# Node attention of a four-layer decoder: the remainders of the rotary angles move from VectorE to GpSimd, ScalarE's folding and sines come a step later

## The chip, the cores and the metric

The kernel runs as one program on one core of a Trainium2 chip. The metric is the device time of one execution in microseconds (us), lower is better. All four compute engines (TensorE, VectorE, ScalarE, GpSimd) and the queue of SyncE run their own instruction streams and meet only at semaphores.

## The reference, cut to what matters

The whole kernel computes a decoder of four layers. The change touches the first attention only, a "node attention" with 16 heads of width 64, 4 groups of keys and values, and 4 nodes. Each token belongs to the 2 nodes of its head with the highest logits. For each node the rotary angle of a token is its count of earlier members times 32 frequencies:

```python
member = one_hot(top_k(x @ wr, 2)).sum(-2) > 0
pos = cumsum(member) - member              # per head and node
for n in range(4):
    c, s = cos(pos[n] * inv_freq), sin(pos[n] * inv_freq)
    qr = q * c + rotate_half(q) * s
    kr = k * c + rotate_half(k) * s
    scores = where(causal & member[n], qr @ kr.T * SCALE, NEG)
    outs.append(softmax(scores) @ v)
y = (softmax(top_k values) * outs at the two chosen nodes).sum()
```

The batch is 4 sequences of 256 tokens, so N = 1024 tokens, S = 256.

## The kernel before, in words

`l0_attn_heads` lays 4 nodes times 32 frequencies on the 128 partitions and the 1024 tokens on the free axis. So a head needs one table of cosines and one of sines, each 128x1024 f32, and both are kept twice (`h % 2`). The loop runs over STEPS = 64 steps, s = 4h + b: head h, sequence b. Every engine has a loop over s of its own, written out by hand, and semaphores that count steps tie them together.

The angles of a head h >= 2 come about in five pieces:

- `turns(h)` (ScalarE, L991): positions times frequency, in full turns, into `cosines`. It is issued at b == 2 of head h - 2, when the tables of that parity are no longer read.
- `reduce_turns(h)` (VectorE, L1063 and L1065): the nearest whole number by adding and subtracting a constant, and the signed remainder, into `sines`. Issued behind `combine` at b == 3 of head h - 2.
- `fold(h)` (ScalarE, L996): absolute value into `cosines`. Issued at b == 3 of head h - 2.
- `sines_of(h)` (ScalarE, L1000 and L1001): two passes of the sine, which need another activation table than the exponents do. Issued at b == 0 of head h - 1.
- The readers: `rotate_q` (VectorE, L1072 to L1082) two steps ahead of the step it serves, so first at b == 2 of head h - 1, and `rotate_k` (GpSimd, L1135 to L1138), which may run up to two steps ahead of the scores. Both wait for `trig_ready`.

In a step s the other work is: VectorE `find_top(s)` (L1088), `rotate_q(s+2)`, `combine(s)` (L1094 to L1105); TensorE `score(s+1)` (L908 to L918, which waits for `combined` of step s - 1, for the rotated keys and the query slots), `weigh(s-2)`, `turn(s-1)` (L928), `project_q(s+3)` (L894); ScalarE `exponents(s)` (L1009), `copy_out(s-2)` (L1024), `copy_turned(s-1)` (L1018). In the last head of a group of four (heads 3, 7 and 11) each step has a K chunk besides: TensorE `project_k` (L886) before `project_q`, and ScalarE `copy_k` (L980), which must be done before TensorE's one projection bank is free for `project_q`.

GpSimd had nothing but `rotate_k`: four instructions a step, of which two are 128x512 and two 128x256.

Of the kernel before, what the change touches and what calls it, by code (L numbers as in the profile page):

```python
# [66 lines left out]
class Core:  # L67
# [12 lines left out]
    def sb(self, name, shape, dt=F32, ctx=None):  # L80
        return (ctx or self.ctx).enter_context(self.nc.sbuf_tensor(name, shape, dt))
# [487 lines left out]
H0, KV0, D0, NODES, CHOICES = 16, 4, 64, 4, 2  # L569
# [3 lines left out]
ROUND = 1.5 * 2.0 ** 23  # L573
# [183 lines left out]
def l0_attn_heads(k, W, values, mix, absent_t, chosen_t, pos_t, heads_t):  # L757
# [3 lines left out]
    nc = k.nc  # L761
# [4 lines left out]
    step = lambda s: divmod(s, B)  # L766
# [9 lines left out]
    with ExitStack() as ctx:  # L776
# [15 lines left out]
        cosines, sines = sb("cosines", [P, 2, N]), sb("sines", [P, 2, N])  # L792
# [25 lines left out]
        with nc.Block() as block:  # L818
# [154 lines left out]
            @block.scalar  # L973
            def _(act):
                def copy_k(chunk):
                    g, (part, half) = chunk // 4, K_CHUNKS[chunk % 4]
                    act.wait_ge(projected_ready, place["k", chunk] + 1)
                    if g >= 1:
                        act.wait_ge(k_rotated, G0 * B * g - 2 + 2 * half)
                    nc.scalar.activation(k_both[:, part, half * BANK:(half + 1) * BANK],  # L980
                                         k_place(chunk), ACT.Copy, scale=D0 ** -0.5)\
                        .then_inc(k_copied, 1)

                def turns(h):
                    if h < 2:
                        act.wait_ge(positions_spread, h + 1)
                    if h >= 2:
                        act.wait_ge(pos_loaded, 64 * (h - 1))
                        act.wait_ge(q_taken, B * (h - 1))
                        act.wait_ge(k_rotated, B * (h - 1))  # L990
                    nc.scalar.activation(cosines[:, h % 2], scores[:, h] if h < 2 else pos[:], ACT.Copy, scale=W("freq"))\  # L991
                        .then_inc(turns_ready, 1)

                def fold(h):
                    act.wait_ge(turns_reduced, h + 1)
                    nc.scalar.activation(cosines[:, h % 2], sines[:, h % 2], ACT.Abs).then_inc(turns_folded, 1)  # L996

                def sines_of(h):
                    act.wait_ge(turns_folded, h + 1)
                    nc.scalar.activation(sines[:, h % 2], sines[:, h % 2], ACT.Sin, scale=-TWO_PI)  # L1000
                    nc.scalar.activation(cosines[:, h % 2], cosines[:, h % 2], ACT.Sin, scale=-TWO_PI,  # L1001
                                         bias=k.quarter_turn[:]).then_inc(trig_ready, 1)

                def exponents(s):
                    for i in range(TB):
                        act.wait_ge(topped, 2 * s + i + 1)
                        for slot in range(CHOICES):
                            one = unit(scores, s, i)[:, slot]
                            last = nc.scalar.activation(one, one, ACT.Exp,  # L1009
                                                        bias=top[:, s % 2, i, slot:slot + 1],  # L1010
                                                        accum_out=total[:, s % 2, i, slot:slot + 1])
                        last.then_inc(exp_ready, 1)

                def copy_turned(s):
                    act.wait_ge(turned_ready, s + 1)
                    if s >= 2:
                        act.wait_ge(out_ready, s - 1)
                    nc.scalar.copy(probs_t[:, s % 2], turned[:, 0:P + S]).then_inc(turned_copied, 1)  # L1018

                def copy_out(s):  # L1020
                    h, b = step(s)
                    part, of = (slice(x % 2 * D0, (x % 2 + 1) * D0) for x in (h, h // G0))
                    act.wait_ge(out_ready, s + 1)
                    nc.scalar.copy(heads_t[part, h // 2, b * S:(b + 1) * S], out_ps[of, s % 2, :])\  # L1024
                        .then_inc(out_copied, 1)

                turns(0)
                turns(1)
                copy_k(0)
                fold(0)  # L1030
                copy_k(1)
                sines_of(0)
                copy_k(2)
                copy_k(3)
                fold(1)
                sines_of(1)
                for s in range(STEPS):
                    h, b = step(s)
                    exponents(s)
                    if s >= 2:  # L1040
                        copy_out(s - 2)
                    if s >= 1:
                        copy_turned(s - 1)
                    if k_chunk_at(s) is not None:
                        copy_k(4 * (s // (G0 * B) + 1) + k_chunk_at(s))
                    if b == 0 and 1 <= h < H0 - 1:
                        sines_of(h + 1)
                    if b == 2 and h + 2 < H0:
                        turns(h + 2)
                    if b == 3 and h + 2 < H0:  # L1050
                        fold(h + 2)
                copy_turned(STEPS - 1)
                copy_out(STEPS - 2)
                copy_out(STEPS - 1)

            @block.vector
            def _(v):
                link = k.vchain

                def reduce_turns(h):  # L1060

                    v.wait_ge(turns_ready, h + 1)
                    link(v, nc.vector.tensor_scalar(sines[:, h % 2], cosines[:, h % 2], ROUND, ROUND, ALU.add,  # L1063
                                                    ALU.subtract))
                    nc.vector.tensor_tensor(sines[:, h % 2], sines[:, h % 2], cosines[:, h % 2], ALU.subtract)\  # L1065
                        .then_inc(turns_reduced, 1)
# [18 lines left out]
                def find_top(s):  # L1085
                    for i in range(TB):
                        v.wait_ge(scores_ready, 2 * s + i + 1)
                        nc.vector.tensor_reduce(top[:, s % 2, i], unit(scores, s, i), AX.X, ALU.max, negate=True)\  # L1088
                            .then_inc(topped, 1)
# [23 lines left out]
                for s in range(STEPS):  # L1113
                    h, b = step(s)
                    find_top(s)
                    if s + 2 < STEPS:
                        rotate_q(s + 2)
                    combine(s)
                    if b == 3 and h + 2 < H0:
                        reduce_turns(h + 2)  # L1120

            @block.gpsimd
            def _(g):
                link = k.gchain

                def rotate_k(s):
                    h, b = step(s)
                    g.wait_ge(k_copied, 4 * (h // G0) + (2 if b < 2 else 4))
                    g.wait_ge(trig_ready, h + 1)
                    if s >= 1:  # L1130
                        g.wait_ge(k_rotated, s)
                    if s >= 2:
                        g.wait_ge(scores_ready, 2 * (s - 1))
                    source = k_both[:, :, of_batch(s)]
                    nc.gpsimd.tensor_tensor(k_part[:], source, at_batch(sines, s), ALU.mult)  # L1135
                    link(g, nc.gpsimd.tensor_tensor(k_rot[:, s % 2], source, at_batch(cosines, s), ALU.mult))  # L1136
                    nc.gpsimd.tensor_tensor(k_rot[:, s % 2, 0], k_rot[:, s % 2, 0], k_part[:, 1], ALU.subtract)  # L1137
                    nc.gpsimd.tensor_tensor(k_rot[:, s % 2, 1], k_rot[:, s % 2, 1], k_part[:, 0], ALU.add).then_inc(k_rotated, 1)  # L1138

                k.gchain(g, nc.gpsimd.memset(spread[:], 0.0))  # L1140
                for h in range(2):
                    nc.gpsimd.affine_select(out=spread[:, h], in_=spread[:, h], compare_op=ALU.not_equal, fill=1.0,
                                            base=-NODES * h, pattern=[[-1, NODES], [0, FREQS]], channel_multiplier=1)\
                        .then_inc(spread_set, 1)
                for s in range(STEPS):
                    rotate_k(s)

# [2408 lines left out]
```

## Time and profile before

| what | value |
|---|---|
| median of 3 runs | 1866.5 us (1866.48 to 1873.33) |
| profiled execution, its own time | 1868.13 us |
| its span, first to last instruction | 1866.4 us |
| busy share of the span | PE 74%, DVE 59%, ACT 38%, POOL 24% |
| stage of the 16 heads | about 38 to 498 us |
| busy in that stage (460.5 us) | PE 394.2, DVE 410.6, ACT 267.4, POOL 267.1 |

The stage is about a quarter of the span. Engine names in the rows: PE is TensorE, PEld its weight loads, DVE VectorE, ACT ScalarE, POOL GpSimd, SP SyncE. A time in brackets behind a row is how long the engine stood idle before it, and who released it. PEclk is the granted TensorE clock as a share of 2.4 GHz. In rows with an x count, start is that of the first and the length covers them all.

### The profile page before, as it was taken

The numbers are of one execution on the slowest core, as the hardware profiler recorded it, in microseconds if no ns is written. First come the engines' busy times: TensorE is split into PE (matmuls) and PEld (weight loads), VectorE is DVE, ScalarE is ACT, GpSimd is POOL, SyncE is SP. The second block draws the span as 40 slices with busy tenths as digits, with TensorE's granted clock in tenths as the row PEclk, the third lists the DMA queues.
The fourth block names the chain that finished last, engine by engine and source line by source line (L and its number), as shares of the span: only waits on it lengthen the run. The fifth ranks groups of instructions, "written<-read, shape, count | busy, mean of one in ns | idle before, by whom it ended". The sixth has DMA issues, their size and how long they took to land. (4 is left out here: it accounts for less than half of the span.)

```text
span 1866.4 us, 25316 instructions
## 1 busy us (share of the span) xinstructions
PE 1387.0 (74%) x9045; PEld 1055.8 (57%) x9045; DVE 1109.8 (59%) x2340; ACT 709.0 (38%) x1529; POOL 443.9 (24%) x464
## 2 busy tenths in 40 slices
PE   4898898888866897774765956758616878869785
PEld 3676666666745564561444955546513756646663
DVE  5899999999446577224566545352454827425534
ACT  4456666656222464221321221013203333634351
POOL 2565566565210100120101310000001015002300
PEclk8899899998878799786887977669868989989897
DMA  6111111010010100430002500000200002000100
GB/s 217 28 35 36 27 41 35 27 41 15 1 58 1 35 1 1 141 116 0 1 13 101 181 17 1 1 1 1 88 3 1 1 1 43 2 0 18 27 2 12
DMA packets 31612, 64.01 MB, mean 34 GB/s; under 512 B 6784, under 2 KB 18176, under 8 KB 30976
## 3 DMA queue, kind: packets, MB, share of 16 engines
q1 hardware_dynamic: 30464, 60.15, 10.4%
q0 software_dynamic: 1024, 2.23, 0.5%
q8 instruction: 74, 1.21, 0.3%
q14 instruction: 50, 0.41, 0.1%
HBM read 54.13 MB, written 4.18 MB: 31 GB/s over the span
## 5 line engine op out<-in xcount | busy, mean ns | idle before, releaser
L188 POOL TENSOR_TENSOR rstd<-spread,minus_half 128x4 f32<-128x4 f32 x36 | 36.9, 1024 | 913.2 <-DVE spread L170 913.2
L918 PE MATMUL l0h_scores<-l0h_k_rot,l0h_q_slots 128*128 128x128 f32 (+1 forms) x1024 | 208.2, 351 | 0.0
L918 PEld LDWEIGHTS l0h_scores<-l0h_k_rot,l0h_q_slots 128*128 128x128 f32 x1024 | 171.2, 210 | 13.3
L1135 POOL TENSOR_TENSOR l0h_k_part<-large_weights,l0h_sines 128x512 f32<-128x512 f32 x64 | 84.0, 1313 | 177.8 <-PE l0h_scores L918 129.8
L1009 ACT ACTIVATE l0h_scores<-l0h_scores,l0h_top 128x128 f32<-128x128 f32 (+1 forms) x256 | 100.6, 393 | 26.3 <-DVE l0h_top L1088 26.2
L1082 DVE TENSOR_TENSOR l0h_q_slots<-l0h_q_rot,l0h_chosen 128x1024 f32<-128x1024 f32 x64 | 78.4, 1225 | 6.7
L894 PE MATMUL l0h_projected<-XT,l0h_wq 128*128 128x256 f32 x256 | 70.1, 397 | 15.8 <-ACT large_weights L980 11.8
L1136 POOL TENSOR_TENSOR l0h_k_rot<-large_weights,l0h_cosines 128x512 f32<-128x512 f32 x64 | 81.0, 1266 | 0.0
L908 PE MATMUL l0h_scores<-l0h_key_masks,l0h_query_picks 4*128 4x128 bf16 (+1 forms) x256 | 45.2, 258 | 47.7 <-DVE l0h_probs L1105 47.7
L1447 ACT ACTIVATE l0n_probs<-l0n_scores,l0n_top 128x256 f32<-128x256 f32 x128 | 53.9, 483 | 38.9 <-DVE l0n_top L1478 38.7
L1088 DVE TENSOR_REDUCE l0h_top<-l0h_scores 128x2 f32<-128x256 f32 (+1 forms) x128 | 65.0, 546 | 5.4 <-PE l0h_scores L918 5.4
L1024 ACT COPY l0a_heads_t<-l0h_out_ps 64x256 f32<-64x256 f32 x64 | 23.5, 367 | 116.9 <-PE l0h_out_ps L939 116.6
L894 PEld LDWEIGHTS l0h_projected<-XT,l0h_wq 128*128 128x128 f32 x256 | 44.6, 194 | 32.6 <-ACT large_weights L980 22.6
L908 PEld LDWEIGHTS l0h_scores<-l0h_key_masks,l0h_query_picks 4*128 4x128 bf16 x256 | 14.1, 93 | 80.4 <-DVE l0h_probs L1105 64.7
L1138 POOL TENSOR_TENSOR l0h_k_rot<-l0h_k_rot,l0h_k_part 128x256 f32<-128x256 f32 x64 | 57.4, 896 | 0.0
L1009 ACT ACTIVATION_READ_ACCUMULATOR l0h_scores<-l0h_scores,l0h_top 128x1 f32 x256 | 52.5, 205 | 0.0
L1072 DVE TENSOR_TENSOR l0h_q_part<-l0h_projected,l0h_sines 128x512 f32<-128x512 f32 x64 | 43.6, 682 | 14.3 <-PE l0h_projected L894 13.8
L1137 POOL TENSOR_TENSOR l0h_k_rot<-l0h_k_rot,l0h_k_part 128x256 f32<-128x256 f32 x64 | 50.1, 784 | 5.0
L1101 DVE TENSOR_SCALAR l0h_probs<-l0h_scores,l0h_share 128x128 f32<-128x128 f32 (+1 forms) x128 | 47.6, 413 | 2.3
L1105 DVE SCALAR_TENSOR_TENSOR l0h_probs<-l0h_scores,l0h_share,l0h_probs 128x128 f32<-128x128 f32 (+1 forms) x128 | 47.5, 413 | 2.3
L2124 POOL DMA_INDIRECT l1e_rows<-l1f_rows,l1e_token_int x16 | 25.6, 1602 | 85.8 <-DVE l1e_token_int L2234 85.2
L1478 DVE TENSOR_REDUCE l0n_top<-l0n_scores 128x4 f32<-128x1024 f32 x32 | 39.1, 1222 | 10.7 <-PE l0n_scores L1399 10.5
(761 smaller groups left out, 3703.6 us busy)
## 6 DMA issues: line engine op xcount, KB each, us to landing
l1e_experts<-in_l_experts SPq DMA_DIRECT2D x16, 768.0 KB, 4.3
l0e_experts<-in_l_experts SPq DMA_DIRECT2D x15, 578.0 KB, 3.9
l0h_chosen<-l0h_chosen_dram SPq DMA_DIRECT2D x64, 128.0 KB, 3.0
small_weights<-in_w_l_ffn SPq DMA_DIRECT2D x1, 4016.0 KB, 12.2
l0h_pos<-l0h_pos_dram SPq DMA_DIRECT2D x56, 64.0 KB, 2.1
large_weights<-in_w_l_xattn SPq DMA_DIRECT2D x1, 2632.0 KB, 9.1
l3f_late<-l3f_values SPq DMA_DIRECT2D x2, 1040.0 KB, 7.0
l0h_wq<-in_l_wq SPq DMA_DIRECT2D x16, 128.0 KB, 3.0
```

The lines of the kernel that those rows point to most:

```text
L894: mm = nc.tensor.matmul(out[:, part * S:(part + 1) * S], wq[:, h % 2, part * P:(part + 1) * P], k.XT[:, b * S:(b + 1) * S], start=True, st ...
L908: nc.tensor.matmul(at[:, slot], query_picks[:, h % 2, slot, query], key_masks[:, h % 2, b * S:b * S + KEYS[i][1]], start=(slot == 0), stop ...
L918: mm = nc.tensor.matmul(at[:, slot], q_slots[:, s % 2, slot, part, i * P:(i + 1) * P], k_rot[:, s % 2, part, 0:KEYS[i][1]], start=False, s ...
L1009: last = nc.scalar.activation(one, one, ACT.Exp, bias=top[:, s % 2, i, slot:slot + 1], accum_out=total[:, s % 2, i, slot:slot + 1])
L1082: nc.vector.tensor_tensor(q_slots[:, s % 2], bc(q_rot[:].unsqueeze(1), [P, CHOICES, 2, S]), chosen_of(s), ALU.mult).then_inc(slots_ready, 1)
L1088: nc.vector.tensor_reduce(top[:, s % 2, i], unit(scores, s, i), AX.X, ALU.max, negate=True)\
L1101: last = nc.vector.tensor_scalar(prob(i), unit(scores, s, i)[:, 0], share[:, s % 2, i, 0:1], None, ALU.mult)
L1135: nc.gpsimd.tensor_tensor(k_part[:], source, at_batch(sines, s), ALU.mult)
L1136: link(g, nc.gpsimd.tensor_tensor(k_rot[:, s % 2], source, at_batch(cosines, s), ALU.mult))
L1137: nc.gpsimd.tensor_tensor(k_rot[:, s % 2, 0], k_rot[:, s % 2, 0], k_part[:, 1], ALU.subtract)
L1138: nc.gpsimd.tensor_tensor(k_rot[:, s % 2, 1], k_rot[:, s % 2, 1], k_part[:, 0], ALU.add).then_inc(k_rotated, 1)
L1447: last = nc.scalar.activation(probs[:, u % 2, o, i], scores[:, u % 2, o, i], ACT.Exp, bias=top[:, u % 2, o, i:i + 1])
```

## The change

Three things move, and nothing is computed differently.

- `reduce_turns` goes from VectorE to GpSimd. It was issued at b == 3 of head h - 2 for head h; now it is issued behind `rotate_k(4(h-1))`, so at b == 0 of head h - 1 in GpSimd's own loop. Heads 0 and 1 stay on VectorE.
- ScalarE's `fold` is issued at b == 0 of head h - 1, where the sines were.
- ScalarE's `sines_of` is issued at b == 1 of head h - 1.

`turns` stays at b == 2 of head h - 2, and all waits keep their counts. For each of the heads 2 to 15 the same instructions run, 14 times in all. In GpSimd's queue `rotate_k(4(h-1)+1)` and all that follows stand behind the two new instructions and their wait for `turns_ready`.

```diff
--- before.py
+++ after.py
@@ -1044,11 +1044,11 @@
                     if k_chunk_at(s) is not None:
                         copy_k(4 * (s // (G0 * B) + 1) + k_chunk_at(s))
                     if b == 0 and 1 <= h < H0 - 1:
+                        fold(h + 1)
+                    if b == 1 and 1 <= h < H0 - 1:
                         sines_of(h + 1)
                     if b == 2 and h + 2 < H0:
                         turns(h + 2)
-                    if b == 3 and h + 2 < H0:
-                        fold(h + 2)
                 copy_turned(STEPS - 1)
                 copy_out(STEPS - 2)
                 copy_out(STEPS - 1)
@@ -1116,8 +1116,6 @@
                     if s + 2 < STEPS:
                         rotate_q(s + 2)
                     combine(s)
-                    if b == 3 and h + 2 < H0:
-                        reduce_turns(h + 2)
 
             @block.gpsimd
             def _(g):
@@ -1137,13 +1135,22 @@
                     nc.gpsimd.tensor_tensor(k_rot[:, s % 2, 0], k_rot[:, s % 2, 0], k_part[:, 1], ALU.subtract)
                     nc.gpsimd.tensor_tensor(k_rot[:, s % 2, 1], k_rot[:, s % 2, 1], k_part[:, 0], ALU.add).then_inc(k_rotated, 1)
 
+                def reduce_turns(h):
+                    g.wait_ge(turns_ready, h + 1)
+                    link(g, nc.gpsimd.tensor_scalar(sines[:, h % 2], cosines[:, h % 2], ROUND, ROUND, ALU.add, ALU.subtract))
+                    nc.gpsimd.tensor_tensor(sines[:, h % 2], sines[:, h % 2], cosines[:, h % 2], ALU.subtract)\
+                        .then_inc(turns_reduced, 1)
+
                 k.gchain(g, nc.gpsimd.memset(spread[:], 0.0))
                 for h in range(2):
                     nc.gpsimd.affine_select(out=spread[:, h], in_=spread[:, h], compare_op=ALU.not_equal, fill=1.0,
                                             base=-NODES * h, pattern=[[-1, NODES], [0, FREQS]], channel_multiplier=1)\
                         .then_inc(spread_set, 1)
                 for s in range(STEPS):
+                    h, b = step(s)
                     rotate_k(s)
+                    if b == 0 and 1 <= h < H0 - 1:
+                        reduce_turns(h + 1)
```

## Rows read from the trace of the kernel before

**Rows 1.** The page's first line: span, and instructions of all engines.
```profile
span 1866.4 us, 25316 instructions
```

**Rows 2.** Windows: 13 heads; one head with K chunks; the next (start:end, length, busy, PEclk).
```profile
98.62:464.18 365.56, 318.30 (x1742) 243.03 (x1741) 337.26 (x704) 224.02 (x610) 218.94 (x208) 0.94 0.11 32
238.89:266.41 27.52, 24.37 (x138) 18.04 (x137) 26.01 (x56) 17.93 (x48) 16.92 (x16) 1.00 0.12 35
266.41:295.25 28.84, 24.77 (x142) 18.62 (x141) 25.44 (x55) 18.00 (x48) 16.92 (x17) 1.00 0.11 34
```

**Rows 3.** Timeline of VectorE, steps 26 to 28 (start, length, engine, line, operation, tiles).
```profile
238.89 0.18 DVE L1094 RECIPROCAL l0h_scores<-l0h_total 128x4 f32<-128x4 f32 x1
...
245.06 0.18 DVE L1094 RECIPROCAL l0h_scores<-l0h_total 128x4 f32<-128x4 f32 x1
...
246.91 0.84 DVE L1063 TENSOR_SCALAR l0h_sines<-l0h_cosines 128x1024 f32<-128x1024 f32 x1
...
247.78 1.63 DVE L1065 TENSOR_TENSOR l0h_sines<-l0h_sines,l0h_cosines 128x1024 f32<-128x1024 f32 x1
...
250.26 0.67 DVE L1072 TENSOR_TENSOR l0h_q_part<-l0h_projected,l0h_sines 128x512 f32<-128x512 f32 x1
...
253.66 0.18 DVE L1094 RECIPROCAL l0h_scores<-l0h_total 128x4 f32<-128x4 f32 x1
```

**Rows 4.** Timeline of TensorE, a plain step, then a step with a K chunk.
```profile
240.88 0.28 PE L908 MATMUL l0h_scores<-l0h_key_masks,l0h_query_picks 4*128 4x128 bf16 x2
...
241.21 1.06 PE L918 MATMUL l0h_scores<-l0h_k_rot,l0h_q_slots 128*128 128x128 f32 x8
...
245.02 0.49 PE L928 MATMUL l0h_turned<-ident,l0h_probs 128*128 128x128 f32 x3
...
245.35 1.03 PE L894 MATMUL l0h_projected<-XT,l0h_wq 128*128 128x256 f32 x4
...
247.04 0.28 PE L908 MATMUL l0h_scores<-l0h_key_masks,l0h_query_picks 4*128 4x128 bf16 x2 [0.67 <-DVE l0h_probs L1105]
...
267.03 0.49 PE L928 MATMUL l0h_turned<-ident,l0h_probs 128*128 128x128 f32 x3
...
269.07 1.13 PE L894 MATMUL l0h_projected<-XT,l0h_wq 128*128 128x256 f32 x4 [0.69 <-ACT large_weights L980]
```

**Rows 5.** Timeline of ScalarE: turns, copies, the sines and what follows them.
```profile
240.49 1.15 ACT L991 ACTIVATE l0h_cosines<-l0h_pos,large_weights 128x1024 f32<-128x1024 bf16 x1
...
245.62 0.48 ACT L1018 COPY l0h_probs_t<-l0h_turned 128x384 f32<-128x384 f32 x1
...
268.42 0.60 ACT L980 ACTIVATE large_weights<-l0h_projected 128x512 f32<-128x512 f32 x1 [0.31 <-PE l0h_projected L886]
...
282.61 1.28 ACT L1000 ACT_TABLE_LOAD   x1
...
284.87 1.13 ACT L1001 ACTIVATE l0h_cosines<-l0h_cosines,quarter_turn 128x1024 f32<-128x1024 f32 x1
...
289.06 0.37 ACT L1024 COPY l0a_heads_t<-l0h_out_ps 64x256 f32<-64x256 f32 x1
```

**Rows 6.** Timeline of GpSimd: one set of rotated keys, and one under the remainders.
```profile
233.77 1.27 POOL L1135 TENSOR_TENSOR l0h_k_part<-large_weights,l0h_sines 128x512 f32<-128x512 f32 x1 [6.24 <-PE l0h_scores L918]
...
237.03 0.73 POOL L1138 TENSOR_TENSOR l0h_k_rot<-l0h_k_rot,l0h_k_part 128x256 f32<-128x256 f32 x1
...
248.29 1.71 POOL L1138 TENSOR_TENSOR l0h_k_rot<-l0h_k_rot,l0h_k_part 128x256 f32<-128x256 f32 x1
```

**Rows 7.** Groups by line and shape, GpSimd, whole span (busy us, mean ns | idle before).
```profile
L2354 POOL MEMSET l2a_values<- 128x7168 f32 x1 | 6.1, 6077 | 12.6 <-POOLq L256 12.6
```

**Rows 8.** Windows: a pause of TensorE in head 6 and the time after it.
```profile
225.40:228.31 2.91, 0.00 (x1) 0.00 (x1) 2.81 (x8) 2.88 (x4) 2.05 (x3) 1.00 0.00 0
228.30:233.80 5.50, 5.49 (x24) 4.25 (x25) 5.19 (x12) 3.79 (x10) 0.03 (x1) 0.69 0.01 5
```

**Rows 9.** Waits of VectorE, 84 to 480 us (us in total, times, longest us).
```profile
DVE l0h_q_part L1072 <- PE l0h_projected L894: 8.5, 11, 1.2
```

## The prediction

> **What bounds the kernel now.** I read the page first for the span [rows 1]; the profiled execution took 1868.1 us, 1.7 more than its span and 1.6 above the median of the runs. The change touches only the 16 heads, so I cut that stage into heads by the windows. From step 6 to step 58, thirteen heads, takes 365.56 us, 28.1 a head. The heads whose last steps carry K chunks (3, 7, 11) take 27.5 each and the ones behind them (4, 8, 12) 28.8 [rows 2], so the other seven take (365.56 - 3 x 27.5 - 3 x 28.8) / 7 = 28.1.
>
> Then the timeline of VectorE, which is busy 337 of those 366 us [rows 2]. I take L1094, the first instruction of `combine`, as the mark of a step and write M(s) for its start. M(26) to M(27) is 6.17 us with no gap: a plain step is VectorE's own work. M(27) to M(28) is 8.60 [rows 3]: the two remainder instructions stand in it. They cost 2.42 us net there, although their own lengths sum to 2.47. Four plain steps and one reduction are 24.68 + 2.42 = 27.1; the other 1.0 of the 28.1 is waiting.
>
> Part of that 1.0 is TensorE's clock. While VectorE reduces, TensorE has nothing to do, and in head 6 it pauses for 2.91 us; in the 5.5 us after the pause its granted clock is 0.69 on the mean, so for (1 - 0.69) / 0.5, about 3.4 us, of it 1.2 GHz [rows 8]. Its projections then come late to `rotate_q`, which waits 8.5 us in 11 waits over the stage [rows 9].
>
> The other engines have slack in a plain step. TensorE needs 5.50 us from the scores to the end of `project_q` (240.88 to 246.38) and then waits 0.67 for `combine` [rows 4]. GpSimd stood idle for 6.24 us before a `rotate_k` of 3.99 us (233.77 to 237.76) [rows 6].
>
> **What is removed.** 14 reductions leave VectorE. If nothing else became late, that is 14 x 2.42 = 34 us. GpSimd gets back little: under VectorE's reduction its L1138 took 1.71 instead of 0.73 [rows 6], beside slack.
>
> **What is added on GpSimd.** Two instructions over 128x1024, which no row shows on that engine. The second has two inputs: L1135 takes 1.27 for 512 columns and L1138 0.73 for 256 [rows 6], so 0.54 per 256 and 0.73 + 3 x 0.54 = 2.35 for 1024. The first has one input: at least as long as a mere write, 6.08 us for 7168 columns or 0.87 for 1024 [rows 7], at most as long as the two-input one, 2.35. I take 1.5, between them. With 0.1 for the link, X = 3.95, call it 4.0, between 3.3 and 4.8.
>
> The Trainium skill's GPSIMD Engine Reference, section Engine selection, advises against such work on this engine: two-input operations are about twice as slow there, while one-input ones run at roughly line rate. The two-input half agrees with the trace, 1.27 on GpSimd against 0.67 for VectorE's 128x512 (L1072). By the one-input half, at that page's 1.2 GHz and one column a cycle, an estimate for the first instruction is 0.85 us and X is 3.3, which would make the sum below about 1858.
>
> **Where it lies: the new chain.** I walk one plain head from M(4h-2) = 0, in the steady state where the sines of the head before came just before it.
>
> 1. ScalarE. The sines end when `rotate_q` can start, 3.4 before the mark (L1072 to L1094, 250.26 to 253.66 [rows 3]). The table load and four exponents end 3.06 later (286.00 to 289.06 [rows 5]), at -0.35; two copies end at 0.5 and `turns` (1.15 [rows 5]) at 1.65.
> 2. GpSimd finished `rotate_k(4h)` at about 0.6 and waits for `turns`. The reduction runs from 1.7 to 5.7, `rotate_k(4h+1)` (4.0) ends at 9.8.
> 3. TensorE would start the key products of `score(4h+1)` at 6.17 + 1.98 + 0.33 = 8.5 (245.06 to 247.04 [rows 3, 4], 240.88 to 241.21 [rows 4]). It waits 1.3. From there to the end of `project_q(4h+3)` is 5.17 (241.21 to 246.38 [rows 4]): 14.97. `rotate_q(4h+3)` wants it at M(4h) + 2.77 = 15.1 (2.77 is 6.17 - 3.40). Just in time: M(4h+1) = 18.5, where before it was 20.9.
> 4. TensorE starts `score(4h+2)` at 14.97 (it could from 14.3) and `turn(4h)` 4.14 later (240.88 to 245.02 [rows 4]), at 19.1. ScalarE's copy ends 1.1 behind that (245.02 to 246.10 [rows 4, 5]) at 20.2. The sines take 3.39 (282.61 to 286.00 [rows 5]) and end at 23.6.
> 5. `rotate_q(4h+4)` on VectorE wanted them at M(4h+1) + 2.77 = 21.3. It waits 2.3, and M(4h+2) = 23.6 + 0.05 + 3.4 = 27.05.
>
> So of the 2.42 that the reduction gives back, about 2.3 is taken by a new wait of L1072 for the sines. The chain closes on itself (mark, turns, remainders, keys, scores, turned probabilities, sines, mark) with a period of 23.05 + X: each us on GpSimd is a us of the head. `fold` (1.06 by the same kind of row) now lies between copies and exponents at about 15 to 16; the exponents end near 17.9, before M(4h+1), so it costs nothing. It would cost if the scores came 0.7 later.
>
> TensorE pauses here too: `project_q(4h+1)` ends at -3.4 + 1.3 + 1.03 = -1.1 and the next scores start at 1.98, a pause of 3.1, no shorter than the 2.91 that was followed by the low clock [rows 8]. So I leave the low clock in. Where it lasts 7 us it delays step 3 by 0.6 to 0.8; where it lasts 3.4 us GpSimd's delay covers it. Mean 0.4: a plain head is 27.45 against 28.1.
>
> **Heads with K chunks.** There a TensorE step is longer by 1.81: from `turn` to the end of the projections 3.17 (267.03 to 270.20) for 1.36 (245.02 to 246.38) [rows 4]. It falls once on step 3, which then also holds up `rotate_q(4h+3)` by 1.8, and the copy of the chunk ends 1.99 behind the start of `turn` (267.03 to 269.02 [rows 4, 5]) for 1.08, so 0.9 more stands ahead of the sines in step 4. The chain is 27.05 + 1.81 + 0.9 = 29.75, with 0.3 for the clock 30.05. Before it was 27.5: there TensorE's long step lay under VectorE's reduction and there was no pause. The heads behind them start with chunks still in steps 2 and 3 (`turns` at 2.3, 0.65 later) but without the 3 us pause: 27.6 against 28.84 [rows 2].
>
> **The sum.** Plain heads, eight with head 1: 8 x (27.45 - 28.1) = -5.2, and +1.0 because head 1 starts without the early `turns` of item 1. Heads 3, 7, 11: 3 x (30.05 - 27.5) = +7.6. Heads 4, 8, 12: 3 x (27.6 - 28.84) = -3.7. A last pause behind head 14: +0.8. Sum +0.5, so the profiled execution would take 1868.6 and the median about 1867 us. With X at 3.3 it is about 14 x 0.7 = 10 less, 1857; with 4.8 it is 14 x 0.8 = 11 more, 1878. The remaining slacks are a few tenths, so half a us a head, 7 us, is my error of the walk itself.
>
> **The rivals.** Effects within 0.5% (9.3 us) can't be told from no change here.
>
> - The forecast, gains and losses cancel, 1867: 0.5, its own range 1860 to 1874.
> - The chain binds less than I think, because the one-input instruction runs at the pace of a write (X 3.3): about 1857. For it: nothing in the instruction needs a second read. Against: two-operation arithmetic is more than a write. 0.15.
> - VectorE stays the bound and all of 34 us comes back: 1833. That needs X under about 1.7, less than the two-input instruction alone. 0.05.
> - GpSimd is slower than I take it, one-input work no faster than two-input or slower: X 4.8 or more, 1878 or more. It decides from X = 4.6. 0.15.
> - The low clock falls on the chain. In step 3 and 4 TensorE's work is 9.3 us of the 27; the 3.4 us of half clock seen in rows 8 cost 1.7 us of work when they lie on it. In the 11 heads with the pause, 11 x 1.7 = 19: 1886. For it: the wait of 1.3 in step 3 makes a second pause. Against: the first pause ends 8 us before the key products, and the second is short. 0.15.
>
> Faster by over 0.5% takes the 0.05, most of the 0.15 at 1857 and a little of the forecast: 0.2. Slower by over 0.5% takes both slow cases: 0.28. The rest, 0.52, is the same. The range 1856 to 1882 holds the forecast, both ends of X and the milder part of the clock's case.
>
> **What would show it.** In the trace after: L1063 and L1065 for heads 2 on stand on POOL, with lengths near 1.5 and 2.35; POOL's wait for L991 ahead of them; L1072 waiting for ACT L1001 about 2.3 us, 14 times, longer in heads 3, 7 and 11; L918 waiting for POOL L1138 about 1.3; L1094 to L1094 at 6.17 but for the step at b == 2 (and b == 1 in the chunk heads); heads of 27.5, of 30 and of 27.6. I am wrong if L1072 doesn't wait for the sines, if X is outside 3.3 to 4.8, or if PEclk in the stage falls well under 0.94.

## The result, and the profile after

The changed kernel took 1912.9 us (median of 4 runs, 1908.7 to 1917.5) beside 1869.9 for the kernel before (1866.5 to 1876.0). The ratio is 1.0227, with a 95% interval of 1.0186 to 1.0267: 2.3% slower, where no change was forecast and the range ended at 1882. Of the runs below, one execution of e11 took 2479.5 us at a granted clock of 0.55; it is in no ratio.

The spans differ by 40.5 us (1866.4 and 1906.9). From M(2) to M(58), the marks between which the moved work lies, the kernel before took 394.2 us and the changed one 433.3: 39.1 of the 40.5 are there. So there is nothing to look for outside the 16 heads. Behind M(63), the mark of the last step, nothing differs between the kernels below, and yet their profiled executions took from 1372.9 to 1381.5 us there; a difference of a few us is therefore read between the marks.

The groups of GpSimd in the changed kernel (mean ns of one behind the busy time; line numbers of `rotate_k` moved to L1133 to L1136):

```profile
L1133 POOL TENSOR_TENSOR l0h_k_part<-large_weights,l0h_sines 128x512 f32<-128x512 f32 x64 | 81.0, 1265 | 133.3 <-ACT l0h_cosines L1001 104.8 <-PE l0h_scores L918 23.7 <-POOL l0h_k_rot L1136 4.8
...
L1140 POOL TENSOR_SCALAR l0h_sines<-l0h_cosines 128x1024 f32<-128x1024 f32 x14 | 50.8, 3631 | 17.7 <-ACT l0h_cosines L991 17.7
...
L1141 POOL TENSOR_TENSOR l0h_sines<-l0h_sines,l0h_cosines 128x1024 f32<-128x1024 f32 x14 | 32.9, 2349 | 1.2
```

The two-input instruction is as predicted, 2.35 us. The one-input instruction takes 3.63 us, not 1.5, and lies outside the bounds of 0.87 and 2.35. X is 6.06, from 196.91 to 202.97 in the next rows, and not 4.0.

One plain head of the changed kernel in the timeline, M(18) to M(22), to be read against the walk and against [rows 3 to 6]:

```profile
195.37 0.18 DVE L1094 RECIPROCAL l0h_scores<-l0h_total 128x4 f32<-128x4 f32 x1
195.68 1.15 ACT L991 ACTIVATE l0h_cosines<-l0h_pos,large_weights 128x1024 f32<-128x1024 bf16 x1
...
196.91 3.63 POOL L1140 TENSOR_SCALAR l0h_sines<-l0h_cosines 128x1024 f32<-128x1024 f32 x1 [0.95 <-ACT l0h_cosines L991]
...
200.62 2.35 POOL L1141 TENSOR_TENSOR l0h_sines<-l0h_sines,l0h_cosines 128x1024 f32<-128x1024 f32 x1
...
206.18 0.72 POOL L1136 TENSOR_TENSOR l0h_k_rot<-l0h_k_rot,l0h_k_part 128x256 f32<-128x256 f32 x1
206.95 1.16 PE L918 MATMUL l0h_scores<-l0h_k_rot,l0h_q_slots 128*128 128x128 f32 x8 [2.09 <-POOL l0h_k_rot L1136]
...
208.48 3.29 PE L918 MATMUL l0h_scores<-l0h_k_rot,l0h_q_slots 128*128 128x256 f32 x8
...
211.81 0.69 DVE L1088 TENSOR_REDUCE l0h_top<-l0h_scores 128x2 f32<-128x512 f32 x1 [1.66 <-PE l0h_scores L918]
213.95 0.69 DVE L1072 TENSOR_TENSOR l0h_q_part<-l0h_projected,l0h_sines 128x512 f32<-128x512 f32 x1 [1.44 <-PE l0h_projected L894]
214.17 1.06 PE L918 MATMUL l0h_scores<-l0h_k_rot,l0h_q_slots 128*128 128x128 f32 x8
...
215.60 1.89 PE L918 MATMUL l0h_scores<-l0h_k_rot,l0h_q_slots 128*128 128x256 f32 x8
217.98 0.49 PE L928 MATMUL l0h_turned<-ident,l0h_probs 128*128 128x128 f32 x3
...
219.08 1.28 ACT L1000 ACT_TABLE_LOAD   x1
...
221.33 1.13 ACT L1001 ACTIVATE l0h_cosines<-l0h_cosines,quarter_turn 128x1024 f32<-128x1024 f32 x1
...
222.57 0.69 DVE L1072 TENSOR_TENSOR l0h_q_part<-l0h_projected,l0h_sines 128x512 f32<-128x512 f32 x1 [2.35 <-ACT l0h_cosines L1001]
...
225.98 0.18 DVE L1094 RECIPROCAL l0h_scores<-l0h_total 128x4 f32<-128x4 f32 x1
```

The chain of the prediction is there link by link: mark, `turns` (ended at 1.5 after the mark, forecast 1.65), GpSimd waiting for it, the remainders, the keys, TensorE waiting for the keys, the sines behind the turned probabilities, and L1072 waiting 2.35 us for them (forecast 2.3). Two links are longer than in the walk: the remainders, and TensorE. From the start of the key products to the end of the scores it took 4.8 us (206.95 to 211.77), where the same matmuls of the next step took 3.3 (214.17 to 217.49), and L1088 waited for it. The windows say why (columns as in [rows 2]):

```profile
69.70:503.00 433.30, 362.74 (x1880) 274.34 (x1878) 333.43 (x729) 240.33 (x658) 300.73 (x252) 0.91 0.10 29
...
202.43:204.86 2.43, 2.43 (x15) 1.71 (x13) 2.32 (x6) 1.55 (x7) 2.43 (x3) 1.00 0.00 0
...
206.95:213.04 6.09, 6.09 (x27) 5.00 (x28) 3.78 (x9) 0.29 (x1) 4.99 (x5) 0.72 0.01 4
```

Before the pause of 2.09 us the granted clock is 1.00; in the 6.1 us behind it 0.72 on the mean, so a good half of them at 1.2 GHz. In the kernel before the clock fell once in a plain head, beside VectorE's work. Here it falls on the chain, at the wait for keys, in 11 of the 14 heads by windows of 2 us. Head 6 is the one plain head where it stayed at 1.00 there, behind a wait of 2.05 us that ended at 237.56:

```profile
235.98:237.98 2.00, 0.41 (x3) 0.42 (x4) 1.79 (x4) 0.44 (x2) 1.69 (x4) 1.00 0.00 0
237.98:239.98 2.00, 2.00 (x15) 1.56 (x14) 1.89 (x6) 0.00 (x0) 2.00 (x2) 1.00 0.00 0
```

It took 28.9 us, the other seven 30.3 to 31.0. The fall behind the first pause of a head, which head 6 has like the others (0.50 from 229.98 to 231.98), so cost it nothing: the chain without low clock is 23.05 + 6.06 = 29.1.

The waits between 84 and 480 us (us in total, times, longest), where the kernel before had 8.5 us in all for L1072 [rows 9]:

```profile
DVE l0h_q_part L1072 <- ACT l0h_cosines L1001: 33.2, 13, 3.3
...
PE l0h_scores L918 <- POOL l0h_k_rot L1136: 23.5, 12, 2.3
DVE l0h_q_part L1072 <- PE l0h_projected L894: 22.1, 16, 3.0
DVE l0h_top L1088 <- PE l0h_scores L918: 20.6, 12, 3.2
```

VectorE waits 33.2 us for the sines, 22.1 for projections and 20.6 for scores; the 14 x 2.42 = 34 us that it no longer works don't cover these.

### The profile page after: what moved, and what is told of

It is laid out like the page before. It is cut to its first block and busy times, and to the rows that moved or that the text cites. A ratio compares the mean times of both kernels' runs of the same rounds, so it can differ in the third digit from the quotient of the medians.

```text
span 1906.9 us, 25316 instructions
## 1 busy us (share of the span) xinstructions
PE 1408.0 (74%) x9045; PEld 1068.6 (56%) x9045; DVE 1080.3 (57%) x2312; ACT 707.8 (37%) x1529; POOL 509.1 (27%) x492
## 5 line engine op out<-in xcount | busy, mean ns | idle before, releaser
L188 POOL TENSOR_TENSOR rstd<-spread,minus_half 128x4 f32<-128x4 f32 x36 | 36.9, 1024 | 913.7 <-DVE spread L170 913.7
L918 PE MATMUL l0h_scores<-l0h_k_rot,l0h_q_slots 128*128 128x128 f32 (+1 forms) x1024 | 223.6, 369 | 29.1 <-POOL l0h_k_rot L1136 29.1
L918 PEld LDWEIGHTS l0h_scores<-l0h_k_rot,l0h_q_slots 128*128 128x128 f32 x1024 | 180.3, 219 | 48.5 <-POOL l0h_k_rot L1136 31.7
L1133 POOL TENSOR_TENSOR l0h_k_part<-large_weights,l0h_sines 128x512 f32<-128x512 f32 x64 | 81.0, 1265 | 133.3 <-ACT l0h_cosines L1001 104.8
L1009 ACT ACTIVATE l0h_scores<-l0h_scores,l0h_top 128x128 f32<-128x128 f32 (+1 forms) x256 | 100.9, 395 | 33.1 <-DVE l0h_top L1088 32.9
L1088 DVE TENSOR_REDUCE l0h_top<-l0h_scores 128x2 f32<-128x256 f32 (+1 forms) x128 | 66.2, 550 | 27.4 <-PE l0h_scores L918 27.4
L1072 DVE TENSOR_TENSOR l0h_q_part<-l0h_projected,l0h_sines 128x512 f32<-128x512 f32 x64 | 44.1, 689 | 64.8 <-ACT l0h_cosines L1001 35.5
L1454 ACT ACTIVATE l0n_probs<-l0n_scores,l0n_top 128x256 f32<-128x256 f32 x128 | 53.8, 483 | 39.1 <-DVE l0n_top L1485 39.0
L1140 POOL TENSOR_SCALAR l0h_sines<-l0h_cosines 128x1024 f32<-128x1024 f32 x14 | 50.8, 3631 | 17.7 <-ACT l0h_cosines L991 17.7
L1009 ACT ACTIVATION_READ_ACCUMULATOR l0h_scores<-l0h_scores,l0h_top 128x1 f32 x256 | 52.8, 206 | 0.0
L1135 POOL TENSOR_TENSOR l0h_k_rot<-l0h_k_rot,l0h_k_part 128x256 f32<-128x256 f32 x64 | 46.4, 725 | 5.0
L1136 POOL TENSOR_TENSOR l0h_k_rot<-l0h_k_rot,l0h_k_part 128x256 f32<-128x256 f32 x64 | 46.4, 725 | 0.0
## 6 DMA issues: line engine op xcount, KB each, us to landing
small_weights<-in_w_l_ffn SPq DMA_DIRECT2D x1, 4016.0 KB, 12.2
```

The lines of the kernel that those rows point to most:

```text
L918: mm = nc.tensor.matmul(at[:, slot], q_slots[:, s % 2, slot, part, i * P:(i + 1) * P], k_rot[:, s % 2, part, 0:KEYS[i][1]], start=False, s ...
L1009: last = nc.scalar.activation(one, one, ACT.Exp, bias=top[:, s % 2, i, slot:slot + 1], accum_out=total[:, s % 2, i, slot:slot + 1])
L1140: link(g, nc.gpsimd.tensor_scalar(sines[:, h % 2], cosines[:, h % 2], ROUND, ROUND, ALU.add, ALU.subtract))
L1454: last = nc.scalar.activation(probs[:, u % 2, o, i], scores[:, u % 2, o, i], ACT.Exp, bias=top[:, u % 2, o, i:i + 1])
```

## The experiments

Three questions: is it the length of the remainders or their place; how much is ScalarE's later place; and is the 1.4 us per head above 23.05 + 6.07 the clock? All ratios below are against the kernel before, run beside them on the same chip. Its medians were 1872.7 (e1 to e4), 1875.0 (e5 to e8) and 1873.6 (e9 to e11).

**e1, the rounding left out.** This kernel does not compute the rounding, and all its remainders are 0.

```diff
-link(g, nc.gpsimd.tensor_scalar(sines[:, h % 2], cosines[:, h % 2], ROUND, ROUND, ALU.add, ALU.subtract))
-nc.gpsimd.tensor_tensor(sines[:, h % 2], sines[:, h % 2], cosines[:, h % 2], ALU.subtract)\
+nc.gpsimd.tensor_tensor(sines[:, h % 2], cosines[:, h % 2], cosines[:, h % 2], ALU.subtract)\
     .then_inc(turns_reduced, 1)
```

> The changed kernel with the first GpSimd instruction (the rounding, 3.63 us) left out and the second one subtracting the angles from themselves, so all remainders are 0: the rounding is not computed. The chain theory (a head lasts 23.05 us plus the time X of the remainders on GpSimd, and the low clock comes on top) has X fall from 6.07 to 2.4 us. GpSimd is then early enough for the scores and TensorE's own order sets the sines: heads of 26.5 to 27 instead of 30.6, so about 50 us less than the changed kernel, near 1862. Rival, the sines' later place alone is the loss: X does not matter, 1905 to 1913. Rival, the low clock is the loss: the pauses before score(4h+4) stay, a gain of at most 15, about 1897.

Measured: 1861.5 us, ratio 0.9947 (0.9928 to 0.9967), 1862 forecast. Plain heads take 26.4 to 26.8 us. The one remaining instruction took 1.90 us, less than 2.35; both its inputs are the same tile. The length of the remainders on GpSimd is what separates the changed kernel from a gain of 0.5%: with short remainders there, the later sines don't make it slow.

**e2, the rounding as two instructions.**

```diff
-link(g, nc.gpsimd.tensor_scalar(sines[:, h % 2], cosines[:, h % 2], ROUND, ROUND, ALU.add, ALU.subtract))
+link(g, nc.gpsimd.tensor_scalar(sines[:, h % 2], cosines[:, h % 2], ROUND, None, ALU.add))
+link(g, nc.gpsimd.tensor_scalar(sines[:, h % 2], sines[:, h % 2], ROUND, None, ALU.subtract))
```

> The changed kernel with the rounding on GpSimd as two instructions, one that adds and one that subtracts, where before one instruction did both. If GpSimd's time in one-input arithmetic goes by operations (two in the 3.63 us), each takes about 1.8 and nothing changes: 1908 to 1916. If one operation runs at the pace of a write (0.87 to 1.0 us), X falls by about 1.6 us, and by the chain theory 14 x 1.6 = 22 us go: about 1890. If the cost goes by instruction, whatever it does, it is 3.6 each and X rises by 3.6: about 1960.

Measured: 1949.9 us, ratio 1.0415 (1.0385 to 1.0444). None of the three forms fits; it is nearest to a cost by instruction. The groups of this kernel, GpSimd:

```profile
L1140 POOL TENSOR_SCALAR l0h_sines<-l0h_cosines 128x1024 f32<-128x1024 f32 x14 | 38.8, 2774 | 17.6 <-ACT l0h_cosines L991 17.6
L1141 POOL TENSOR_SCALAR l0h_sines<-l0h_sines 128x1024 f32<-128x1024 f32 x14 | 38.8, 2774 | 1.2
```

One operation with a constant takes 2.77 us, the two in one instruction 3.63: the second operation costs 0.86 and the rest of the instruction 1.9. X is about 8.1 here, 2.0 more than in the changed kernel, and 14 x 2.0 = 28 of the 37 us follow from it. No run separated the rest; the granted clock from M(2) to M(58) is 0.87 here and 0.91 in the changed kernel.

**e3, ScalarE's part alone.** On the kernel before, VectorE reducing at b == 3:

```diff
                     if b == 0 and 1 <= h < H0 - 1:
+                        fold(h + 1)
+                    if b == 1 and 1 <= h < H0 - 1:
                         sines_of(h + 1)
...
-                    if b == 3 and h + 2 < H0:
-                        fold(h + 2)
```

> ScalarE's part alone: remainders on VectorE at b == 3 as in the kernel before, fold at b == 0 and sines at b == 1. The walk gives the sines ready at 25.4 us after the mark where rotate_q wants them at 23.7: L1072 waits 1.7 in every head, heads of about 28.9 instead of 28.1, 10 us slower than the kernel before, about 1878. Rival, GpSimd's time is the whole loss and ScalarE's place costs nothing: 1866 to 1870. Rival, ScalarE's later place is most of the loss: 1900 or more.

Measured: 1903.7 us, ratio 1.0163 (1.0137 to 1.0189), three times the forecast loss, and where the rival stood by which ScalarE's later place is most of the loss (1900 or more). The wait is the forecast one but longer, in this kernel's list of waits (98 to 500 us):

```profile
DVE l0h_q_part L1072 <- ACT l0h_cosines L1001: 36.5, 14, 4.5
```

That is 2.6 a head for 1.7. At 187.14 us, in a head where the clock was full, the wait is 1.68, as walked; in others it is up to 4.5. A part that I had not seen: `rotate_k` of the next head now starts with the late sines and so falls on VectorE's reduction. L1065 takes 1.84 us on the mean instead of 1.50, and the step with the reduction 9.0 to 9.6 in ten of the 14 heads; in the kernel before it was 8.6 in nine of them [rows 3]. So ScalarE's half costs 30 us when VectorE keeps the remainders, while e1, with the same place of the sines and no reduction on VectorE, is faster than the kernel before: what the later sines cost depends on which engine has the remainders.

**e4, the second keys first.** The same instructions, one place later in GpSimd's loop:

```diff
                     rotate_k(s)
-                    if b == 0 and 1 <= h < H0 - 1:
+                    if b == 1 and 1 <= h < H0 - 1:
                         reduce_turns(h + 1)
```

> The changed kernel with the remainders behind the second set of rotated keys of the head (b == 1 in GpSimd's loop) instead of the first. Same instructions, same total time on GpSimd. The chain theory: the keys of step 4h+1 are ready before TensorE wants them, the remainders end at about 10.7 us after the mark, long before the fold at 16, and the keys of step 4h+2 are just in time. The remainders leave the chain: heads of 26.5 to 27, about 50 us less than the changed kernel, near 1860, so below the kernel before. Rival, what counts is how much GpSimd has to do: 1905 to 1913. Rival, the delay moves on to the keys of step 4h+2: 1885 to 1900.

Measured: 1861.7 us, ratio 0.9949 (0.9926 to 0.9973), 1860 forecast. Since GpSimd does the same work for the same 6.07 us, the loss needs the place of it too: in front of the keys that TensorE wants next. Of VectorE's large waits in the changed kernel only the one for the sines is left (84 to 480 us):

```profile
DVE l0h_q_part L1072 <- ACT l0h_cosines L1001: 29.1, 14, 3.3
DVE l0h_q_part L1072 <- PE l0h_projected L894: 7.6, 9, 1.3
...
DVE l0h_top L1088 <- PE l0h_scores L918: 0.8, 3, 0.3
```

**e5, and the sines ahead of the copies.** On e4, in ScalarE's loop:

```diff
                     exponents(s)
+                    if b == 1 and 1 <= h < H0 - 1:
+                        sines_of(h + 1)
                     if s >= 2:
                         copy_out(s - 2)
...
-                    if b == 1 and 1 <= h < H0 - 1:
-                        sines_of(h + 1)
```

> e4 with one thing more: at b == 1 ScalarE issues the sines right behind the exponents, ahead of copy_out and copy_turned, so that they no longer wait for TensorE's scores and turned probabilities. In e4 L1072 still waits 1.8 us for the sines in each head (27.4 us in 13 waits). The chain theory: the sines end about 2.4 us earlier, before L1072 wants them, and a plain head falls from 26.7 to 24.7 to 25.3, four plain steps of VectorE: 20 to 28 us less than e4, about 1837. Rival, the copies that now come behind the sines hold up TensorE and the turned probabilities, and the wait only moves there: no gain, 1855 to 1865.

Measured: 1834.4 us, ratio 0.9786 (0.9758 to 0.9815), 1837 forecast: 2.1% faster than the kernel before, and the best of all. VectorE's timeline over one head has no gap:

```profile
198.34 0.17 DVE L1094 RECIPROCAL l0h_scores<-l0h_total 128x4 f32<-128x4 f32 x1
...
204.51 0.17 DVE L1094 RECIPROCAL l0h_scores<-l0h_total 128x4 f32<-128x4 f32 x1
...
223.04 0.17 DVE L1094 RECIPROCAL l0h_scores<-l0h_total 128x4 f32<-128x4 f32 x1
```

Each step of this head is 6.17 or 6.18 and a plain head 24.7, VectorE's own work, which the rival at 1833 stood for; it is reached here with X at 6.07, because X is off the chain. The granted clock from M(2) to M(58) is 1.00, and TensorE's longest pause there is 0.8 us.

**e6, the sines early with the remainders left in place.** The edit of e5 on the changed kernel.

> The changed kernel with the sines right behind the exponents at b == 1, and the remainders left where the change put them. The chain then runs turns, remainders (6.07), keys (4.1), scores of step 4h+1 (3.3), copies, fold and exponents (4.9), sines (3.4), rotate_q: about 27 us instead of 29.1, and less of it is TensorE's: about 45 us less than the changed kernel, 1865 to 1875. Rival, TensorE's late scores set the head whatever ScalarE does: 1900 or more.

Measured: 1906.0 us, ratio 1.0175 (1.0146 to 1.0205): my forecast missed by 30 us, and the rival holds. L1072 no longer waits for the sines, and TensorE's wait for keys grows to up to 3.5:

```profile
PE l0h_scores L918 <- POOL l0h_k_rot L1136: 41.9, 13, 3.5
DVE l0h_top L1088 <- PE l0h_scores L918: 41.3, 13, 3.8
DVE l0h_q_part L1072 <- PE l0h_projected L894: 29.5, 22, 3.0
```

I had closed the chain over the sines, but a shorter loop lies inside it: mark, `turns`, remainders, keys, scores, projection, `rotate_q(4h+3)`, and then a plain step to the next mark. With early sines `turns` also ends 2.0 after the mark instead of 1.5, since VectorE no longer waits for the sines just before the mark. The keys come 12.2 after the mark, so this loop is 12.2 + 5.17 + 3.4 + 6.17 = 26.9. Plain heads take 28.7 where the clock is at 0.5 for about 3.5 us behind the wait for keys, and 30.1 to 30.2 where it is for about 7: half of that time more, as TensorE's share of the loop runs at half speed.

**e7 and e9, the pauses filled.** Matmuls whose result nobody reads, on the changed kernel:

```diff
+def fill(n, copied):
+    pe.wait_ge(turned_copied, copied)
+    for _ in range(n):
+        nc.tensor.matmul(turned[:, P + S:BANK], k.ident[:], k.ident[:], start=True, stop=True, ...)
...
+                        if i == 0 and b == 1 and h >= 1:      # e9: h % 4 in (1, 2)
+                            fill(14, s - 2)                   # e9: fill(9, s - 2)
                         if i == 0:
                             pe.wait_ge(k_rotated, s + 1)
...
+                    if s % B == B - 1 and 1 <= s // B < H0 - 1:   # e9: the same heads
+                        fill(12, s - 1)
                     if s + 1 < STEPS:
                         score(s + 1)
```

> The changed kernel with useless matmuls into unused columns of the turned bank: 12 before the scores of each step 4h+4, 14 before the key products of each step 4h+1, in the pauses of TensorE. They compute nothing that is used. If the 1.4 us by which heads exceed 23.05 + 6.07 = 29.1 are the low clock, the granted clock in the stage rises from 0.91 to nearly 1.0 and heads fall to about 29.2: some 15 us less, 1895 to 1900. Rival, the 1.4 us are a wait that the walk missed: clock up and time unchanged, 1908 to 1916.

> e7 with the useless matmuls in the plain heads alone (1, 2, 5, 6, 9, 10, 13, 14) and 9 instead of 14 before the key products of step 4h+1, so that they end before the keys do. In e7 plain heads fell from about 30.6 to 29.47, with the 14 ending 0.65 us behind the keys, and the other heads rose. If the low clock is what plain heads have above 23.05 + 6.07, they take 29.0 to 29.4 here and the whole is 8 x 1.2, some 10 us, less than the changed kernel: 1900 to 1905. Rival, the gain in plain heads is eaten in the heads behind them: 1908 to 1916.

e7: 1910.3 us, ratio 1.0203 (1.0170 to 1.0237), not to be told from the changed kernel, though its granted clock rose from 0.91 to 1.00. By the whole time the rival would have it. The heads say otherwise. Head lengths, worked out as the difference of the starts of L1094 at b == 2, means:

```
                         plain (8)   3, 7, 11   4, 8, 12
changed kernel             30.4        32.1       31.4
e7, 14 and 12 everywhere   29.4        32.0       32.6
e9, 9 and 12 in plain      29.0        32.6       31.4
```

In e7 the matmuls take about 8 us off the eight plain heads and add 4 in heads 4, 8 and 12; from M(2) to M(58) e7 is 3.9 us shorter than the changed kernel (429.4), and behind M(58) 4 us longer, 1.8 of them in the last head, which hides it in the whole time. e9 leaves them out in the other heads and takes 1900.8 us, ratio 1.0146 (1.0113 to 1.0179), as forecast, with plain heads at 29.0 where the chain without low clock gives 29.1. The low clock is 1.4 us of a plain head of the changed kernel.

**e8, the sines at b == 0 again.**

```diff
-                    if b == 1 and 1 <= h < H0 - 1:
+                    if b == 0 and 1 <= h < H0 - 1:
                         sines_of(h + 1)
```

> The changed kernel with ScalarE's sines put back to b == 0, behind the fold, GpSimd as in the change. By the walk the fold ends at about 18.3 us, the sines at 21.7 and the exponents of step 4h+1 behind the second table load at 24.8, which VectorE wants at 18.5 to 20.5: the exponents become the wait in place of L1072, heads of 31 to 32, slower than the changed kernel by 10 to 20, about 1925. Rival, the later place of the sines is what the change loses: then this gains 20 or more, under 1890.

Measured: 1965.0 us, ratio 1.0494 (1.0457 to 1.0530), in the forecast direction but 40 us more. The exponents became the wait (L1094 for L1009, 36.9 us in 11), and TensorE waited longer for keys (49.9 us in 12), with the clock at 0.84 between 100 and 460 us. With the remainders on GpSimd where the change put them, the later place of the sines is needed.

**e10, the walk at a size within its bounds.** Rounding and remainders are not computed here; two instructions of a length between the bounds stand in their place.

```diff
-link(g, nc.gpsimd.tensor_scalar(sines[:, h % 2], cosines[:, h % 2], ROUND, ROUND, ALU.add, ALU.subtract))
-nc.gpsimd.tensor_tensor(sines[:, h % 2], sines[:, h % 2], cosines[:, h % 2], ALU.subtract)\
+link(g, nc.gpsimd.tensor_tensor(sines[:, h % 2], cosines[:, h % 2], cosines[:, h % 2], ALU.subtract))
+nc.gpsimd.tensor_tensor(sines[:, h % 2], sines[:, h % 2], cosines[:, h % 2], ALU.mult)\
```

> The changed kernel with two two-input instructions on GpSimd in place of the rounding and the difference: a subtraction of the angles from themselves (1.90 us in e1) and a product (2.35), so X is 4.35 and all remainders are 0 (rounding and remainders are not computed). This is the prediction's walk at a size inside its own bounds. If only the size of X was wrong, its sum holds here: 1867 + 14 x 0.35, about 1872, heads of 27.4 to 27.9. If the low clock on TensorE's share of the chain was missed as well, plain heads are 28.5 to 29 and the time 1882 to 1890.

Measured: 1873.1 us, ratio 0.9999 (0.9978 to 1.0021), with 1.90 and 2.36 us on GpSimd. Heads took 27.8 (plain), 30.3 (3, 7, 11) and 27.7 (4, 8, 12); the walk with 0.35 more has 27.8, 30.4 and 27.95. The prediction's sum holds where its size does, though the 27.8 is in part luck: it is the mean of six plain heads at 26.9 to 27.2, below the chain's 27.4 without low clock, and of heads 1 and 13 at 30.6 and 28.8. In these two and in head 7 TensorE waited 1.2 to 1.8 us for keys and the granted clock fell to 0.5; so the last rival's case turned up in three heads even with X in its bounds. The walk also makes this kernel 5 us slower than the kernel before, and the two were alike (1873.1 and 1873.6).

**e11, without GpSimd.** ScalarE's order of e5 with the remainders on VectorE.

> The kernel before with ScalarE's part of e5 alone: fold at b == 0, sines at b == 1 right behind the exponents; the remainders stay on VectorE at b == 3. A plain head is then 4 x 6.17 + 2.42 = 27.1 plus what the low clock costs, against 24.7 in e5: 1855 to 1865, so that the remainders on GpSimd, behind the second set of keys, are worth 25 us of e5. Rival, the order on ScalarE is the whole gain of e5: 1835 to 1842.

Measured: 1865.4 us, ratio 0.9963 (0.9945 to 0.9982), at the edge of the forecast 1855 to 1865. Plain heads are mostly 27.3, so the move to GpSimd in the right place is worth 31 us of e5 (1865.4 less 1834.4).

## Why the prediction was wrong, point by point

**The step that failed** is the bound in "What is added on GpSimd": the one-input instruction "at most as long as the two-input one, 2.35". It measured 3.63. X was 6.06 and not 4.0, and 14 x 2.1 = 29 of the 43 us follow from it by the prediction's own rule, that each us on GpSimd is a us of the head. In e10, with X inside the bounds, the rest of the sum comes out as far as the heads show it, with the luck told there. That upper bound had no row behind it; here the instruction with fewer inputs was the longer one. The Trainium skill's GPSIMD Engine Reference, section Engine selection, has one-input work at roughly line rate. The estimate of 0.85 us from it went further the same way; the measurement, 3.63 us, decides against it.

**The second term**, the low clock on the chain, was the last rival. Its condition, that the wait for keys makes a second pause behind which the clock falls, was judged at a wait of 1.3 us; with X at 6.06 the wait was 2.09 and the clock fell in 11 of 14 heads. It measured 1.4 us in a plain head (e9). The sum had 0.4 for the clock, and put it behind the first pause, where it cost nothing (head 6). The walk with X at 6.06 gives 29.5, 32.1 and 29.7 for plain heads, for 3, 7, 11 and for 4, 8, 12; they took 30.4, 32.1 and 31.4. That makes 28 of the 39.1 us between the marks; of the other 11, 6 are in the plain heads and 5 in heads 4, 8 and 12. In these three the clock fell at the wait for keys too; in e10, where it did not, they took 27.7 for the walk's 27.95. The run that filled the pause in these three (e7) also put matmuls where they have none, so for them the clock is argued and not shown.

**Right:** the chain and its order, `turns` early behind a waiting VectorE, L1072's wait of 2.3 for the sines, TensorE's wait for L1136, VectorE's 6.17 a step, fold hidden, GpSimd's two-input instruction at 2.35, the longer heads 3, 7 and 11. The rival "GpSimd slower than I take it" named X from 4.8 up at 1878 or more; its end was open and its chance of 0.15 too small for a term with no row of its kind. That the forecast of 1867 stood beside the rivals at 0.5 rested on the 1.5 for the one-input instruction, the middle of two bounds of which the upper was wrong.

**Missed besides:** a loop inside the loop. e6 showed that taking the sines off the chain gains little, since the keys alone hold a head at 28.7 to 30.2. The place behind the second keys (e4) opens the inner one, and with early sines (e5) both are open.

What stays open is why the clock did not fall at the wait for keys in heads 6 and 11, whose waits (2.05 and 1.77 us) were like the others' (1.83 us in head 9, where it fell); in head 7 the wait was only 0.65. No run separated this. e3's loss has two parts that were read from its trace, the wait and the slower reductions, and neither was tried alone.

## What to carry to other kernels

Work moved to an engine with idle time is put in front of something in that engine's queue, and what counts is who waits for that something and by when: the same two instructions went with a loss of 2.3% in front of the next keys, with a gain of 0.5% behind them, and with 2.1% when ScalarE's order was changed as well. Where a periodic chain closes, its period is the sum of its links, so an unmeasured length on it enters once per turn; take the upper bound of an instruction that no row shows from work of its kind, not from work that merely looks harder. And a new wait on TensorE in such a chain can cost twice, as here in 11 of 14 heads: once as the wait and once as the slower clock behind it.

## What the runs showed of the hardware

- GpSimd, 128x1024 f32: one operation with a constant 2.77 us, two in one instruction 3.63, a difference of two tiles 2.35, of a tile with itself 1.90. So here an instruction with one input and constants is slower than one with two inputs. VectorE takes 0.69 for the same two operations when GpSimd is idle (L1063 for heads 0 and 1).
- TensorE's clock fell to 1.2 GHz at waits for keys of 1.8 to 3.5 us in 11 of 14 heads, in four of them (1, 4, 8 and 12) with no fall earlier in the head; with the pauses filled (e7) or gone (e5) it stayed at 1.00 from M(2) to M(58). The low clock was 1.4 us of a plain head of 30.4 (e9).
- VectorE's L1065 (two inputs, 128x1024 f32) takes 1.22 us when it starts with GpSimd idle, and 1.63 (kernel before) to 2.27 (e3) when an instruction of `rotate_k` is already running; GpSimd's L1138 takes 1.71 under it instead of 0.73 [rows 6].
